# Eight tensor-scalar operations in place of VectorE's pair comparison, placed between its other work

## What is computed

```python
# layer 1, relational, per edge e with source s, destination t, relation r
msg   = sum_b w_comp[r, b] * (x[s] @ weight[b])
a     = tanh(relu(sum((x[s] @ A1.T + b1) * (x[t] @ A2.T + b2 + rel_emb[r])) / sqrt(32)))
nei   = segment_sum(a * msg, t)
h     = relu(nei + x[s of the last edge into t] @ self_loop_weight)   # 0 without edges
x     = layernorm(x + h)
# layer 2: segment_sum(x[src], dst); layer 3: softmax-weighted sum over edges; layer 4: ten steps of
# f = 0.9 * norm * segment_sum(f[src] * norm, dst) + 0.1 * x
```

## Time and profile before

| What | us |
|---|---|
| Median of the 3 runs shown (1175.4 to 1184.0) | 1178.94 |
| The profiled execution's own time | 1179.21 |
| Its span, first to last instruction | 1177.4 |
| Mean granted TensorE clock | 0.866 of full |

### The profile page before, as it was taken

How to read it: one execution, slowest core, us unless ns; L and a number is a source line. 1 busy time by engine, 2 the same in 40 slices (tenths; PEclk the granted TensorE clock), 3 DMA queues, 4 the chain that set the end, 5 groups by cost and what they waited for, 6 DMA issues and landing times.

```text
span 1177.4 us, 55398 instructions
## 1 busy us (share of the span) xinstructions
PE 896.5 (76%) x23682; PEld 846.3 (72%) x23682; DVE 929.4 (79%) x1684; ACT 507.7 (43%) x1244; POOL 640.4 (54%) x580
## 2 busy tenths in 40 slices
PE   3358887868688768776787777767376968999996
PEld 2357877767587667776776677766376968999996
DVE  8869999978798879887888787887647996555556
ACT  0235655444554447664756566656458410000000
POOL 5777777777777777777777787877000000000000
PEclk9568999987798889888878888889587989999998
DMA  4432322322233223222322223231000000000001
GB/s 114 60 72 55 63 59 54 64 55 45 51 56 55 53 45 60 49 53 50 60 47 54 49 55 62 44 55 29 4 3 2 4 3 4 4 5 4 4 5 18
DMA packets 54911, 47.93 MB, mean 41 GB/s; under 512 B 35966, under 2 KB 45182, under 8 KB 54662
## 3 DMA queue, kind: packets, MB, share of 16 engines
q0 software_dynamic: 18176, 9.34, 9.7%
q1 hardware_dynamic: 30822, 14.16, 5.8%
q10 hardware_dynamic: 5664, 20.84, 4.8%
HBM read 41.98 MB, written 2.31 MB: 38 GB/s over the span
## 4 chain that ended last, share of the span: by engine, by line
POOL 42%; PE 23%; DVE 16%; issue 15%; DMA 2%; ACT 2%; DVEq 0%; ACTq 0%; SPq 0%
POOL arena L633 42%; PE ps L885 13%; PE ps L932 3%; DVE arena L1373 2%; PE ps L916 2%; PE ps L856 2%; PE ps L895 2%; DVE aggT L1417 1%; DMA arena<-line_table 1%; ACT arena L1122 1%; DVE arena L1368 1%; DVE arena L1404 1%; DMA arena<-rel_rows_in 1%; DVE arena L1388 1%; PE ps L818 0%
## 5 line engine op out<-in xcount | busy, mean ns | idle before, releaser
L633 POOL DMA_INDIRECT arena<-x_pad,arena x568 | 638.5, 1124 | 173.4 <-issue 173.1
L818 PE MATMUL ps<-aggT 128*128 128x128 f16 x3024 | 230.1, 247 | 44.3 <-DVE aggT L1417 44.3
L818 PEld LDWEIGHTS ps<-aggT 128*128 128x128 f16 x3024 | 216.5, 114 | 49.0 <-DVE aggT L1417 49.0
L1404 DVE TENSOR_TENSOR arena<-ps,arena 128x1536 f32<-128x1536 f32 x98 | 172.4, 1759 | 3.4
L885 PE MATMUL ps<-arena,adj_words 128*128 128x64 f16 x5625 | 171.9, 192 | 3.3 <-DVEq L1666 3.2
L885 PEld LDWEIGHTS ps<-arena,adj_words 128*128 128x128 fp8e4 x5625 | 170.5, 97 | 4.6 <-DVEq L1666 3.5
L1075 ACT ACTIVATE adj_words<-arena 128x500 uint8 x196 | 126.5, 645 | 56.6 <-ACT arena L1050 54.9
L780 PE MATMUL ps<-arena 128*32 128x44 f32 (+4 forms) x7048 | 134.5, 215 | 20.2 <-DVE arena L1404 20.0
L1045 ACT ACTIVATE arena<-ps 128x500 fp8e4<-128x500 f32 x196 | 113.0, 577 | 79.0 <-PE ps L767 79.0
L780 PEld LDWEIGHTS ps<-arena 128*32 128x32 f32 x7048 | 110.5, 115 | 43.8 <-DVE arena L1404 26.7
L1373 DVE TENSOR_TENSOR arena<-pair_no,arena 128x2400 bf16<-128x2400 f16 x98 | 137.3, 1401 | 0.0
(11 more groups left out here) (222 smaller groups left out, 1153.2 us busy)
## 6 DMA issues: line engine op xcount, KB each, us to landing
arena<-line_table ACTq DMA_DIRECT2D x48, 344.0 KB
arena<-x_pad,arena POOLq DMA_INDIRECT x568
arena<-pick_table SPq DMA_DIRECT2D x27, 256.0 KB
arena<-line_table ACTq DMA_DIRECT2D x48, 80.0 KB
arena<-dst_parts SPq DMA_DIRECT2D x196, 5.7 KB
agg_table<-arena SPq DMA_DIRECT2D x196, 2.5 KB
dst_parts<-aggT SPq DMA_DIRECT2D x1, 735.0 KB
x<-x_pad SPq DMA_DIRECT2D x1, 400.0 KB
```

The lines of the kernel that those rows point to most:

```text
L633: pool.indirect_dma_start(to, None, table, bass.IndirectOffsetOnAxis(ap=index, axis=0)).then_inc(done, 16)
L818: mm = nc.tensor.matmul(ps[:, at:at + PICK_WIDE * FEAT], pick_hot[:, u % PICK_RING, k * P:(k + 1) * P], x_parts[:, t, j * PICK_WIDE:(j + 1 ...
L1404: v.tensor_tensor(mixed[:, d % 2, :, :, 0:BASES], fetched_of(d)[:, :, SCORED:REL_COLS].unsqueeze(2).to_broadcast(n), weighted.unsqueeze(3) ...
```

## The change

The single comparison of L1373 becomes eight tensor-scalar operations, one per slot of the duo, each over just the columns that `count` uses, with the slot's pair number as a float32 scalar of each partition. `pair_of` takes the place of `pair_twice` (same size), and the copy of L1292 goes. The comparisons are issued in runs of three, three and two: after the product, after the sum, and after the row comparison. Where an operation's result is read by the next, the wait (`chain.wait`) is moved behind the comparisons in between. In a duo with a picked read the order is mask, rows, adds of halves, last two pairs, add of the pairs. One unit's `pick_hot` comes ahead of the last-edge comparison and the others between the weighted one-hot and the mixed product. `make_lines` moves behind the mixed product. The wait for `pairs_used` comes ahead of the first pair comparison, right behind the product; the row comparison has none of its own.

```diff
-        dst_off, last_off_1 = [stay.cut(GROUPS * SLOTS).rearrange("p (g k) -> p g k", k=SLOTS) for _ in range(2)]
-        pair_twice = stay.cut(2 * GROUPS * SLOTS, F16).rearrange("p (g k i) -> p g k i", k=SLOTS, i=2)
+        pair_of, dst_off, last_off_1 = [stay.cut(GROUPS * SLOTS).rearrange("p (g k) -> p g k", k=SLOTS) for _ in range(3)]
...
-            link(v.tensor_copy(pair_twice, pair_whole.unsqueeze(3).to_broadcast([P, GROUPS, SLOTS, 2])))
...
-                def make_pairs(d):
-                    h = d % 2
-                    if d >= 2:
-                        dve.wait_ge(pairs_used, (d - 1) * DUO)
+                def make_rows(d):
                     n = [P, WIDE, P // 2, 2]
-                    v.tensor_tensor(row_hot[:, h].rearrange("p k (v i) -> p k v i", i=2),
+                    v.tensor_tensor(row_hot[:, d % 2].rearrange("p k (v i) -> p k v i", i=2),
...
-                    n = [P, WIDE, HOTS * BLOCKS // 2, 2]
-                    v.tensor_tensor(pair_hot[:, h].rearrange("p k (v i) -> p k v i", i=2),
-                                    pair_no[:].rearrange("p (v i) -> p v i", i=2).unsqueeze(1).to_broadcast(n),
-                                    slots_of(pair_twice, d).rearrange("p g k i -> p (g k) i").unsqueeze(2).to_broadcast(n),
-                                    ALU.is_equal).then_inc(pairs_ready, 1)
+
+                def make_pairs(d, k0, k1):
+                    if k0 == 0 and d >= 2:
+                        dve.wait_ge(pairs_used, (d - 1) * DUO)
+                    for k in range(k0, k1):
+                        n = PAIR_DSTS[k % SLOTS] * BLOCKS
+                        last = v.tensor_scalar(pair_hot[:, d % 2, k, 0:n], pair_no[:, 0:n],
+                                               pair_of[:, d * DUO + k // SLOTS, k % SLOTS:k % SLOTS + 1], None, ALU.is_equal)
+                    if k1 == WIDE:
+                        last.then_inc(pairs_ready, 1)
...
                 for d in range(DUOS):
-                    score_edges(d)
-                    if d + 1 < DUOS:
-                        make_pairs(d + 1)
-                    c = d // LINE_DUOS
+                    c, own = d // LINE_DUOS, UNITS_AT.get(d, [])
+                    picked_now, more = PICK_READ_AT.get(d), d + 1 < DUOS
+                    products_of(d)
+                    if more:
+                        make_pairs(d + 1, 0, 3)
+                    scores_of(d)
+                    if more:
+                        make_pairs(d + 1, 3, 6)
+                    if picked_now is not None:
+                        mask_picked(picked_now)
+                    if more:
+                        make_rows(d + 1)
+                    if picked_now is not None:
+                        add_halves()
+                    if more:
+                        make_pairs(d + 1, 6, WIDE)
+                    if picked_now is not None:
+                        add_pairs(picked_now)
+                    if d % LINE_DUOS == 1 and c + 1 < LINES:
+                        make_dst_hot(c + 1)
+                    for n in own[0:1]:
+                        make_pick_hot(*n)
+                    make_last(d)
+                    weigh(d)
+                    for n in own[1:]:
+                        make_pick_hot(*n)
+                    make_mixed(d)
                     if d % LINE_DUOS == 0 and c >= 1 and c + 1 < LINES:
                         make_lines(c + 1)
-                    if d % LINE_DUOS == 1 and c + 1 < LINES:
-                        make_dst_hot(c + 1)
-                    if d in PICK_READ_AT:
-                        read_picked(PICK_READ_AT[d])
-                    for c, j in UNITS_AT.get(d, []):
-                        make_pick_hot(c, j)
-                    make_mixed(d)
```

More of the change, by code:

```diff
@@ L296, in gnn @@
         dst_t, next_t = [of.bitcast(I32).rearrange("p (g k) -> p g k", k=SLOTS) for of in (dst_words, next_words)]
-        pair_whole = next_words.rearrange("p (g k) -> p g k", k=SLOTS)
         block_of = prep.cut(GROUPS * SLOTS, I32).rearrange("p (g k) -> p g k", k=SLOTS)
@@ L1289, in _ @@
             link(v.tensor_tensor(last_off_1, dst_t, next_t, ALU.not_equal))
-            link(v.scalar_tensor_tensor(out=pair_whole, in0=dst_off, scalar=float(BLOCKS), in1=block_of,
+            link(v.scalar_tensor_tensor(out=pair_of, in0=dst_off, scalar=float(BLOCKS), in1=block_of,
                                         op0=ALU.mult, op1=ALU.add))
-            link(v.tensor_copy(pair_twice, pair_whole.unsqueeze(3).to_broadcast([P, GROUPS, SLOTS, 2])))
             link(v.scalar_tensor_tensor(out=last_off_1, in0=dst_off, scalar=1.0, in1=last_off_1, op0=ALU.add, op1=ALU.mult))
@@ L1380, in fetched_of, with products_of @@
                     return ps[:, at:at + WIDE * REL_COLS].rearrange("p (k c) -> p k c", k=WIDE)
-                def score_edges(d):
+                def products_of(d):
                     dve.wait_ge(fetched, d + 1)
@@ L1387, in score_edges, with scores_of, make_last @@
                         dve.wait_ge(gathered[d % AHEAD], 16 * tiles)
-                    link(v.tensor_tensor(product, fetched_of(d)[:, :, 0:SCORED], xp[:, d % AHEAD], ALU.mult))
+                    step(v.tensor_tensor(product, fetched_of(d)[:, :, 0:SCORED], xp[:, d % AHEAD], ALU.mult))
+                def scores_of(d):
+                    chain.wait()
                     v.tensor_reduce(score[:, d % 2, :], product, AX.X, ALU.add).then_inc(score_ready, 1)
-                def make_mixed(d):
-                    at = d % LINE_DUOS * WIDE
-                    own_hot = dst_hot[:, d // LINE_DUOS % 2, at:at + WIDE, :]
+                def make_last(d):
                     if d >= 2:
@@ L1399, in make_mixed, with weigh @@
                                     ALU.is_equal)
+                def weigh(d):
+                    at = d % LINE_DUOS * WIDE
                     dve.wait_ge(weight_ready, d + 1)
-                    link(v.scalar_tensor_tensor(out=weighted, in0=weight_e[:, d % 2, :].unsqueeze(2).to_broadcast(n),
-                                                scalar=0.0, in1=own_hot, op0=ALU.max, op1=ALU.mult))
+                    step(v.scalar_tensor_tensor(out=weighted,
+                                                in0=weight_e[:, d % 2, :].unsqueeze(2).to_broadcast([P, WIDE, HOTS]), scalar=0.0,
+                                                in1=dst_hot[:, d // LINE_DUOS % 2, at:at + WIDE, :], op0=ALU.max, op1=ALU.mult))
+                def make_mixed(d):
+                    chain.wait()
                     n = [P, WIDE, HOTS, BASES]
@@ L1418, in make_pick_hot, with mask_picked @@
                      .then_inc(pick_hots, 1)
-                def read_picked(c):
+                picked_of = picked.rearrange("p (k w f) -> p k w f", k=WIDE, w=PICK_WIDE)
+                def mask_picked(c):
                     dve.wait_ge(pick_used, PICK_DEEP * (c + 1))
                     n = [P, WIDE * PICK_WIDE, FEAT]
-                    link(v.tensor_tensor(picked.rearrange("p (w f) -> p w f", f=FEAT),
+                    step(v.tensor_tensor(picked.rearrange("p (w f) -> p w f", f=FEAT),
                                          ps[:, PICK_AT_BANK:PICK_AT_BANK + WIDE * PICK_WIDE * FEAT]
@@ L1426, in read_picked, with add_halves @@
                                          pick_mask[:, c].rearrange("p k w -> p (k w)").unsqueeze(2).to_broadcast(n), ALU.mult))
+                def add_halves():
+                    half = PICK_WIDE // 2
+                    chain.wait()
                     dve.sem_inc(pick_read, 1)
-                    of = picked.rearrange("p (k w f) -> p k w f", k=WIDE, w=PICK_WIDE)
-                    half = PICK_WIDE // 2
-                    link(v.tensor_tensor(of[:, :, 0:half], of[:, :, 0:half], of[:, :, half:PICK_WIDE], ALU.add))
@@ L1431, in read_picked, with add_pairs @@
-                    link(v.tensor_tensor(xp[:, PICKED[c] % AHEAD, :, 0:FEAT], of[:, :, 0, :], of[:, :, 1, :], ALU.add))
+                    step(v.tensor_tensor(picked_of[:, :, 0:half], picked_of[:, :, 0:half], picked_of[:, :, half:PICK_WIDE], ALU.add))
+                def add_pairs(c):
+                    chain.wait()
+                    step(v.tensor_tensor(xp[:, PICKED[c] % AHEAD, :, 0:FEAT], picked_of[:, :, 0, :], picked_of[:, :, 1, :], ALU.add))
                 make_lines(0)
                 make_dst_hot(0)
-                make_pairs(0)
+                make_rows(0)
@@ L1436, in run_sweep @@
+                make_pairs(0, 0, WIDE)
                 make_lines(1)
                 for d in range(DUOS):
-                    score_edges(d)
-                    if d + 1 < DUOS:
-                        make_pairs(d + 1)
-                    c = d // LINE_DUOS
+                    c, own = d // LINE_DUOS, UNITS_AT.get(d, [])
[25 more added lines that the diff above has]
+                    make_mixed(d)
```

## The result

The changed kernel takes **1148.24 us** (median of 4, 1147.47 to 1148.61) against 1180.76 us before, a ratio of **0.9725 (95% interval 0.9697 to 0.9754)**. That is 32.5 us less. The forecast was 1140 us, with a range of 1108 to 1180.

The account below looks back on a forecast made before the run. GpSimd's gathers bound the kernel, with 101.5 us of stretch. Remaining terms 6.6 + 17.9 + 16 + 13 + 8 = 61.5 us, so 1179.2 - (101.5 - 61.5) = 1139.2, said as 1140 us; range 1108 to 1180.

Parts of the forecast that it names:

- The gather sets the end: GpSimd's 568 gathers set the end; beyond 0.945 us each they are stretched by 101.5 us.
- L1373 held 44.4 us at the start and 26.1 behind it: Sweep gathers meeting the long pair comparison: 44.4 us waiting for its end would go, 26.1 behind it mostly too.
- An operation that is in flight about 0.13 us after a gather's start holds it: On VectorE beside GpSimd's gathers: such an operation holds the gather until that operation is over.
- Cost on VectorE: Eight short comparisons take 1.59 us per duo, 0.27 more than now; filled waits give 0.34 back, 7 us less in all.
- The short ones hold by chance, 16 us: In the sweep 113 of 525 gathers meet a short comparison and wait 0.14 us each, 16 us.
- I keep 8 for runs that end in an L1417: Later stretch, 26.1 us behind L1373, mostly goes; 8 us stay for short runs ending in a unit's comparison.
- Row comparison, 17.9 us "left": The 57 sweep gathers that meet the row comparison L1368 keep their 17.9 us of stretch.
- The sum: Whole kernel: stretch falls from 101.5 to 61.5 us, so 1179.2 becomes 1139.2, said as 1140 us.
- Rival two: Late pairs in 27 picked duos delay TensorE, at most 51 us: 1165; chance 0.24 together with rival four.
- Rival three: Each run of short comparisons holds the gather as one block: stretch 135.5 us, time 1213; chance 0.13.
- Rival one: Better phase in the sweep, fewer gathers meet anything: stretch 35 us, time 1113; chance 0.13.
- Rival four: L1368 and L1417 take L1373's place as holder, stretch near 101 us: 1179; chance 0.24 together with rival two.

Follow-up runs that it names:

- the swap: Changed kernel with the row comparison right behind the sum and the second run of three short comparisons behind it: 1135.68 us, ratio 0.9619.
- second experiment: Kernel before, with only the pair comparison split into eight short ones in one run at its old place, old order and waits kept: 1146.72 us, ratio 0.9712.

## Why the prediction was right, and where a term was off

- **The gather sets the end, at 0.945 us each plus stretch.** Right. The gain of the profiled execution (30.6 us) is the stretch that went (31.7) but for 1 us, and the experiment without comparisons moves with its stretch too.
- **L1373 held 44.4 us at the start and 26.1 behind it.** Right in kind: the split alone gives 1146.72. The Trainium skill's inference that the prediction weighed ("SBUF — State Buffer", section "Who interferes with whom": a tensor-tensor operation doesn't stop descriptor generation) does not hold for this gather. Replacing that operation by tensor-scalar ones took 31 us of stretch away, where by that inference 16 us would have come on top.
- **"An operation that is in flight about 0.13 us after a gather's start holds it."** Too wide, and the count by chance rests on it. In the kernel before, 152 gathers met L1404, which reads PSUM, 34 the sum (L1389) and 28 the last-edge comparison of 96 elements (L1397), and lost 0.3 us together. The operation must also have begun before the gather, as the next point shows.
- **Cost on VectorE, 1.59 us per duo for the eight, 0.34 given back.** Right: the short ones last 285 ns in the median (forecast 260 to 290) and follow each other 0.20 us apart (three last 0.68, one 0.29). From its first product to the end of the sweep VectorE spent 737.7 us, less 69.0 of waits for rows, tanh and fetched factors, 668.7; before 765.8 less 90.6, 675.2: 6.5 us less, I had 7.
- **The short ones hold by chance, 16 us.** Oversized: 4.6 us. Beside 150 gathers a short one is in flight 0.13 us after the start, but 78 of these aren't stretched at all. 76 of the 78 met an operation that had begun less than 0.05 us ahead of the gather, or after it; the 68 that a short one did hold all met one begun at least 0.045 us ahead. The gather at 82.92 us, for one, lasts 0.94 us beside a run begun at 82.88. An operation of 0.285 us that must have begun 0.05 ahead and still run 0.13 behind leaves a window of 0.1 us in place of 0.285, and half of that as mean wait; by this estimate 784 of them in some 720 us hold 11% of 524 gathers for 3 us. Of L1373's 1.40 us the same rule takes 0.18 off.
- **"I keep 8 for runs that end in an L1417."** This is the term that failed: the later part measured 35.9 us. I had looked only at runs of tensor-scalar operations. Some 17 us of it come from gathers that meet the last short comparison and are let go only behind the row comparison; the swap took 11.4 us of stretch and 12.6 us of time away. Another 12.3 come from the line comparison in its new place behind the mixed product. No run moves that alone; with the lines cut in four, no gather that meets the mixed product is stretched.
- **Row comparison, 17.9 us "left".** It fell to 8.3 of direct hold and 4.1 later, and holds others as a neighbour.
- **The sum.** The stretch is 70.0 us where I had 61.5, and the tail between the last gather and the sweep's end is 1.5 us longer (16.7 for 15.3). That the forecast came within 8 us is in part luck: the later part was 27.9 us too low, the short ones 11.4 and the row comparison 9.6 too high, and they cancel for the most part. The gain of L1373's 44.4 us was the sound part of it.
- **Rival two, late pairs.** TensorE's wait rose as it said, by 29 us; GpSimd's idle time stayed its own issue, and what the tail gained, 1.5 us, is about all that it can have cost. **Rival three, blocks by run:** fell with the run of eight, though the neighbour of another kind shows that a hold can outlast the operation that it meets. **Rival one** needed 35 us of stretch, which not even the kernel without any pair comparison had (44.1). **Rival four**, L1373's place taken by others and the stretch near 101, fell with the 70.0.

## What to carry to other kernels

An engine at 80% busy is not the bound when another runs without a gap: look for the stream whose only idle time is issue, and at the distance between its median and its mean. In this kernel GpSimd's gathers pay for the length of VectorE's long tensor-tensor and tensor-scalar operations on SBUF and for which two of them stand side by side, so cut and reorder those while VectorE still waits for something. When its wait is nearly gone, stop: with 14.7 us left, a cut that added 27 us of busy time cost 11.

## What the runs showed that I had not expected

- A gather that meets a short tensor-scalar operation is let go at its end if another tensor-scalar one follows (the gather at 373.61 us), but 28 gathers were held 0.6 us longer by a tensor-tensor operation of 1024 elements that had begun 0.1 us ahead of that end. One swap in the order gave 12.6 us.
- Other pairs stand in the traces. Held through as well: 7 gathers that met a short one ahead of the destination offsets' comparison (second experiment), and 3 and 6 that met one ahead of the add of halves (lines cut; lines and rows cut). Let go at the end of the first: all 55 that met the row comparison ahead of L1373 in the kernel before, though both read SBUF alone, and 3 that met a short one ahead of the mask (L1432), which reads PSUM, in the changed kernel. So the second operation's operands matter and the first one's kind seems to, but not alone: two halves of the row comparison held 10 gathers of 21 through, those where the second half began 0.07 us after the gather's start, and not those where it began at 0.28.
- Which lock or queue makes these differences stays open: the runs show the end times, not the mechanism, and no run was made for one pair alone.
